# Graph-network layers on one core: VectorE adds two slots of a gathered group onto two others before TensorE sums them

## The reference

```python
msg = jnp.concatenate([h[src], h[dst]], axis=-1) @ Mw.T + Mb
deg = jax.ops.segment_sum(jnp.ones((msg.shape[0],), msg.dtype), dst, num_segments=N)
s1 = jax.ops.segment_sum(msg, dst, num_segments=N)
s2 = jax.ops.segment_sum(msg * msg, dst, num_segments=N)
mx = jax.ops.segment_max(msg, dst, num_segments=N)
mn = jax.ops.segment_min(msg, dst, num_segments=N)
mean = s1 / deg[:, None]
var = jax.nn.relu(s2 / deg[:, None] - mean * mean)
std = jnp.sqrt(var + STD_EPS)
agg = jnp.concatenate([mx, mn, std, var], axis=-1)
h_neigh = jnp.concatenate([agg, agg * (logd / DELTA), agg * (DELTA / logd)], axis=-1)
u = jnp.concatenate([h, h_neigh], axis=-1) @ Uw.T + Ub
# batch norm over nodes, mixing product, leaky ReLU, + h; then layer norm and ELU
```

## Time and profile before

| | us |
|---|---|
| median of 3 runs | 2186.88 (2179.98 to 2197.56) |
| the profiled execution, its own time | 2167.94 |
| its span, first to last instruction | 2166.1 |
| TensorE, VectorE, ScalarE, GpSimd busy | 1219.2, 710.3, 313.7, 1286.6 |

### The profile page before, as it was taken

One profiled execution on the slowest core, in us unless ns is written; L12 is line 12 of the kernel. 1 busy time (PEld: TensorE's weight loads), 2 busy tenths in 40 slices (PEclk: granted clock), 3 DMA queues, 4 the chain that ended last, 5 costly groups with the idle time before them and its releaser, 6 DMA issues.

```text
span 2166.1 us, 14665 instructions
## 1 busy us (share of the span) xinstructions
PE 1219.2 (56%) x4692; PEld 874.3 (40%) x4692; DVE 710.3 (33%) x1711; ACT 313.7 (14%) x807; POOL 1286.6 (59%) x1344
## 2 busy tenths in 40 slices
PE   6520675655546683175575637485156556646585
PEld 5310453444434452153453525353145344434452
DVE  8800423333222352042232413253033223223344
ACT  0110410110000144010100100035011000000015
POOL 2756477666766406666666666604757767667604
PEclk9995788777777796587786868697578878678798
DMA  6253233333333213323233333203323333233300
GB/s 61 70 147 92 59 97 92 89 87 94 98 84 92 61 46 115 92 85 95 88 94 94 87 95 92 86 27 116 104 73 93 94 89 96 86 92 95 92 10 30
DMA packets 88488, 183.62 MB, mean 85 GB/s; under 512 B 31790, under 2 KB 47489, under 8 KB 88409
## 3 DMA queue, kind: packets, MB, share of 16 engines
q0 software_dynamic: 61264, 164.22, 26.8%
q1 hardware_dynamic: 27150, 18.51, 3.9%
HBM read 169.06 MB, written 14.98 MB: 85 GB/s over the span
## 4 chain that ended last, share of the span: by engine, by line
another core or an unknown queue 46%; PE 28%; issue 12%; ACT 7%; DVE 5%; POOL 1%; DMA 0%; SPq 0%; DVEq 0%; ACTq 0%; POOLq 0%
PE ps L689 12%; PE ps L712 7%; PE ps L699 2%; ACT base L830 1%; PE ps L709 1%; PE ps L674 1%; PE ps L754 1%; PE ps L639 1%; PE ps L719 1%; PE ps L739 1%; ACT msq L846 1%; ACT u_sb L863 1%; ACT agg L850 0%; ACT base L828 0%
## 5 line engine op out<-in xcount | busy, mean ns | idle before, releaser
L548 POOL DMA_INDIRECT G<-p_by_rank,index x812 | 796.0, 980 | 525.6 <-issue 227.4
L689 PE MATMUL ps<-G,wide_ident 128*128 128x256 f32 x2436 | 634.6, 410 | 19.8 <-DMA G<-p_by_rank,index 12.2
L689 PEld LDWEIGHTS ps<-G,wide_ident 128*128 128x128 f32 x2436 | 499.5, 209 | 122.1 <-issue 17.5
L548 POOL DMA_INDIRECT G<-p_by_node,index x406 | 399.7, 985 | 217.5 <-issue 129.3
L712 PE MATMUL ps<-w_u_sb,aggT 128*128 128x384 f32 x600 | 266.6, 598 | 217.8 <-issue 137.0
L1261 DVE SCALAR_TENSOR_TENSOR u_sb<-ps,amp,u_sb 128x128 f32<-128x128 f32 x75 | 26.3, 351 | 824.4 <-ACT u_sb L863 599.7
L712 PEld LDWEIGHTS ps<-w_u_sb,aggT 128*128 128x128 f32 x600 | 137.9, 236 | 341.8 <-issue 200.8
L699 PE MATMUL ps<-wide_ident,agg 128*128 128x128 f32 x300 | 61.3, 339 | 339.8 <-ACT agg L850 254.2
L699 PEld LDWEIGHTS ps<-wide_ident,agg 128*128 128x128 f32 x300 | 42.2, 171 | 364.3 <-ACT agg L850 268.7
L719 PE MATMUL ps<-wide_ident,u_sb 128*128 128x128 f32 x75 | 23.8, 318 | 181.9 <-DVE u_sb L1263 101.2
L1140 DVE TENSOR_TENSOR acc<-G 128x512 f32<-128x512 f32 x150 | 96.4, 684 | 39.7 <-DMA G<-p_by_rank,index 38.5
(11 more groups left out here) (202 smaller groups left out, 1158.0 us busy)
## 6 DMA issues: line engine op xcount, KB each, us to landing
G<-p_by_rank,index POOLq DMA_INDIRECT x812
G<-p_by_node,index POOLq DMA_INDIRECT x406
p_by_rank<-base SPq DMA_DIRECT2D x12, 512.0 KB, 3.0
p_by_node<-G SPq DMA_DIRECT2D x6, 514.0 KB
w_u_sb<-in_w_u SPq DMA_DIRECT2D x3, 768.0 KB
x_r<-rows_by_rank SPq DMA_DIRECT2D x1, 1600.0 KB
windows<-src_pad SPq DMA_DIRECT2D x1, 1118.0 KB, 25.1
index<-rows_by_rank SPq DMA_DIRECT2D x1, 468.0 KB
```

Source lines behind the costliest of these rows:

```text
L548: g.indirect_dma_start(G[:, n % R, j, 0:w], None, table, bass.IndirectOffsetOnAxis(ap=index[:, t, k0 + j:k0 + j + 1], axis=0))\
L689: ins = mm(out_ps, ident[:, :], G[:, n % R, k, 0:2 * D], start=False, stop=n in END and k == nk - 1)
```

## The change

VectorE gets a new step `fold` right behind `compare`: for each group of more than two slots it adds slots 2 and 3 (or slot 2 alone of three) onto slots 0 and 1 in place, all 256 columns, once its own comparison of that group is complete. TensorE then sums at most two slots a group, and waits for the fold (`groups_folded`) before it. The first groups of a tile are folded only when the first comparison of that tile is made, which is at its second group, or at its third where the second is an odd rest (j == 1 + rest). TensorE's and ScalarE's steps at e + 4 move to e + 5, VectorE's `combine` from e + 4 to e + 5, `statistics` from e + 6 to e + 8.

```diff
--- before.py
+++ after.py
@@ -110,6 +110,7 @@
     END = {tile_groups[t][-1]: t for t in range(T)}
+    FOLD = {n: i for i, n in enumerate(n for n in range(NG) if GROUPS[n][3] > 2)}
@@ -316,6 +317,7 @@
+        folded = Signal(sem("groups_folded"), len(FOLD))
@@ -684,10 +686,13 @@
+                if n in FOLD:
+                    pe.wait_ge(folded.sem, folded.at(l, FOLD[n] + 1))
                 pe.wait_ge(gathered[n % R].sem, gathered[n % R].at(l, slot_before[n]))
-                for k in range(nk):
+                left = min(nk, 2)
+                for k in range(left):
                     ins = mm(out_ps, ident[:, :], G[:, n % R, k, 0:2 * D],
-                             start=False, stop=n in END and k == nk - 1)
+                             start=False, stop=n in END and k == left - 1)
                 ins.then_inc(pe_used.sem, 1)
@@ -720,13 +725,13 @@
-                for n in range(NG + 5):
+                for n in range(NG + 6):
                     if n < NG:
                         sums(l, n)
...
-                    if n - 4 in END:
-                        turn_update(l, END[n - 4])
+                    if n - 5 in END:
+                        turn_update(l, END[n - 5])
                     if n - 2 in END:
                         update(l, END[n - 2])
@@ -870,9 +875,9 @@
-                for n in range(NG + 5):
-                    if n - 4 in END:
-                        copy_update(l, END[n - 4])
+                for n in range(NG + 6):
+                    if n - 5 in END:
+                        copy_update(l, END[n - 5])
@@ -1161,6 +1166,20 @@
+            def fold(l, n):
+
+                t, j, _, nk = GROUPS[n]
+                own = tile_groups[t]
+                rest = GROUPS[own[1]][3] < GW
+                if j <= rest or n not in FOLD:
+                    return
+                dve.wait_ge(dve_used.sem, dve_used.at(l, n + 1))
+                for g in own[0:j + 1] if j == 1 + rest else [n]:
+                    if g in FOLD:
+                        more = GROUPS[g][3] - 2
+                        TT(G[:, g % R, 0:more, 0:2 * D], G[:, g % R, 0:more, 0:2 * D],
+                           G[:, g % R, 2:2 + more, 0:2 * D], ALU.add).then_inc(folded.sem, 1)
@@ -1274,11 +1293,11 @@
-                for n in range(NG + 7):
-                    if n - 6 in END:
-                        statistics(l, END[n - 6])
-                    if n - 4 in END:
-                        combine(l, END[n - 4])
+                for n in range(NG + 9):
+                    if n - 8 in END:
+                        statistics(l, END[n - 8])
+                    if n - 5 in END:
+                        combine(l, END[n - 5])
                     if n - 1 in END:
                         variance(l, END[n - 1])
@@ -1286,6 +1305,7 @@
                         compare(l, n)
+                        fold(l, n)
                         if n in CLOSE:
                             close(l, n)
                         if n in END:
```

## The result

The changed kernel takes 2204.97 us (median of 20 runs, 2193.05 to 2217.87) where the kernel before takes 2186.8 (20 runs beside them): ratio **1.0081, interval 1.0058 to 1.0104**. The forecast was 2147. The time went the wrong way. The change is under 1%, but with twenty runs of each kernel its interval excludes no change at all.

A forecast was written before the change was run, and what follows sets the result against it. GpSimd's gather stretches, 81% of the span, were taken as the bound, with 154 us of ring waits winnable. Terms -48 + 17 - 9 = -40 us gave 2147 us from 2186.9; range 2060 to 2240.

The forecast's parts named there:

- Fewer sums, -48: TensorE's sums: 31% fewer records make its steps less late, shrinking 154 us of GpSimd's ring waits in proportion, -48 us.
- Folds, +17: VectorE's folds beside the gathers: up to 202 us more busy time slows gathers by 0.082 us per us, +17 us.
- fourth rival: Gathers beside folds: each fold holds a gather by 0.519 us, +96 in all, 2283 us; chance 0.04.
- New waits, 0: TensorE's sums waiting for VectorE's folds at a tile's first groups: priced at 0 while GpSimd is ahead.
- third rival: A tile's first groups: folds tie TensorE to VectorE, the 154 us grow by 51, total 2246 us; chance 0.18.
- Later steps, 0: Update's turn, combination and statistics moved to later groups: 0 us of their own.
- The layer's end, -9: After a layer's last gather: 20 fewer products gain 9.9 us, ten folds partly fit idle time; -3 a layer, -9.
- second rival: Lateness of TensorE's steps: the number of products does not matter, +8 in all, 2195 us; chance 0.18.

The follow-up runs named there:

- e18: Kernel before with TensorE adding only the first slot of each group, no fold, on a chip with late TensorE steps: 2134.72 us against 2177.24, ratio 0.9815.
- e1: Kernel before with TensorE adding only the first two slots of a group, no fold, on a chip with prompt steps: 1883.78 us, ratio 0.9992.
- e13: Kernel before with TensorE adding only the first slot of each group, no fold, on a chip with prompt steps: 1886.94 us, ratio 0.9998.
- e5: The changed kernel itself, run again against the kernel before on a chip with prompt steps: 1905.23 us, ratio 1.0102.
- e3: Kernel before plus 98 fold-shaped VectorE additions a layer on data of their own, TensorE not waiting for them, prompt steps: 1899.42 us, ratio 1.0073.
- e14: Changed kernel with VectorE's running minima in PSUM, against the kernel before, prompt steps: 1884.57 us, ratio 0.9986.
- e10: Kernel before with VectorE's running maxima in PSUM for all but the last tile, prompt steps: 1886.88 us, ratio 0.9995.
- e11: Kernel before with VectorE's running minima, the second comparison of each pair, in PSUM, prompt steps: 1864.08 us, ratio 0.9873.
- e9: Changed kernel without the additions: VectorE only steps the folds' semaphore, TensorE waits for it and adds all slots; prompt steps: 1891.97 us, ratio 1.0011.
- e6: Kernel before with two slots summed a group, later steps and VectorE additions on separate data, no wait for folds, prompt steps: 1903.81 us, ratio 1.0095.
- e2: Kernel before with only the later steps, no fold, all slots summed by TensorE, prompt steps: 1885.9 us, ratio 0.9999.
- e17: Changed kernel without folds in a layer's last three tiles, ScalarE's tile 22 copy held until the layer's last gather issues, late steps: 2186.73 us, ratio 1.0009.
- e16: Changed kernel with ScalarE's copy of tile 22's turned aggregates held until the layer's last gather issues, late steps: 2202.75 us, ratio 1.0060.
- e15: Kernel before with ScalarE's copy of tile 22's turned aggregates held until the layer's last gather issues, late steps: 2192.64 us, ratio 1.0013.
- e12: Kernel before with running minima in PSUM and each tile's first minimum made by a copy to PSUM, prompt steps: 1854.65 us, ratio 0.9824.
- e8: Kernel before plus 98 VectorE additions a layer at the folds' places, of a constant to one SBUF tile, prompt steps: 1882.75 us, ratio 0.9984.

## Why the prediction was wrong

*Fewer sums, -48.* This is the step that failed: I let the lateness of TensorE's steps shrink in proportion to its records. In e18 48% fewer records left ScalarE's late steps at 986 us (939 before) and took 29 us from the stretches, where my proportion has 74. Scaled down to 31% of the records that is 29 x 31/48 = 19 us, an estimate, where steps are late; by e1 and e13 it is nothing where they are prompt. Rows 8 did order the lateness by records, weakly, as I wrote; I took the proportional value all the same. In the changed kernel even the 19 us do not show: GpSimd's waits rose by 21.

*Folds, +17.* Right in size with prompt steps: the stretches grew by 15 us (e5), the folds alone cost 13 to 21 (e3, e14). But that was luck: I priced by busy time, which e10 refutes. A fold that began ahead of a gather costs what is left of it 0.13 us after the gather's start, else nothing; over 294 folds that came to 0.05 us each, near the low end. The Trainium skill ("SBUF — State Buffer", "Who interferes with whom") has an instruction with two SBUF inputs contend with GpSimd's reads, and lets the order of issue decide which of the two blocks. The traces agree on both: a gather behind such an instruction is held to its very end, 780 times out of 780, near the boundary the instruction is lengthened instead, and 112 meetings with one input from SBUF in e11 held none. My fourth rival read that rule as a hold for every fold; in e5 87 of 294 folds held a gather, for 0.16 us in the mean. In the first pair of traces the holds did not grow (near 42 us both before and after): 9.7 us of folds came in, and other instructions of VectorE held less. That is an observation; no run shows why.

*New waits, 0.* Right with prompt steps (e9: 1.0011 with an interval from 1.0000; e6 equals e5). Where steps are late, TensorE does wait for folds (466 us, 122 of them in the second layer's gather stretch) and VectorE for the squared mean (longest wait 25.8), as the third rival has it. But GpSimd's waits rose by 21 us and not by 51. No run took the link away on a late chip, so its share there stays open.

*Later steps, 0.* Right by themselves with prompt steps (e2).

*The layer's end, -9.* Wrong in sign with prompt steps, and most likely with late ones. I counted the 20 products as gained and let the folds fit an idle place. With prompt steps the ends grow by 2 us each (e5), by additions and later steps together (e6). With late steps they grew by 10 each in the first pair of traces, and e17 against e16 puts the folds of the last three tiles at 13 us (5 to 20) of the whole time. Against that, the ends in the traces of e15 and e16 sum to 131 and 128 us. The first pair of traces overstates the growth: the span before (2166.1) lies below all timed runs of its kernel, that of after near the top of its own.

So the account of the measured +18, with late steps, is this. The folds at the layers' ends cost some 13 us (e17 against e16). All the rest comes to nothing within the noise (e17 against the kernel before: 1.0009), which must be terms that nearly cancel: fewer products, holds and waits for folds. Their sizes were not separated. With prompt steps the change costs 19 us, and the traces show it: holds +15, ends +6. The second rival (2195) came nearest to 2205 on the faster side, though it has the layer's end with the wrong sign.

Open: why TensorE's steps are late on some chips at all, whether it belongs to the chip or to something else in those runs, what the link costs there, and how e12 does there; it was run with prompt steps alone.

## What to carry over

Beside a stream of GpSimd's gathers, price a VectorE instruction by whether its two inputs lie in SBUF and whether it is already under way when a gather starts, not by its busy time. Putting one input in PSUM on the instruction that is caught won 1.3% (e11); taking nearly half the products of the sums from TensorE, which is off the path with prompt steps, won nothing (e1). An experiment that changes an instruction's inputs must keep its length and its place, or it tells nothing of the inputs (e8). A late step that no row explains should not be priced in proportion to anything: look first whether it occurs on another chip. When work is moved between engines, follow the stretch in which nothing covers the new wait.

## What the runs showed of the hardware

- The GpSimd instruction that gathers 128 rows takes 0.946 us (median of e2, e5 and after). If a VectorE instruction with two SBUF inputs began at least 0.045 us ahead of it and is under way 0.13 us after its start, it takes longer by what is left of that instruction: 780 of 780 cases in three traces, the longest gather 1.48 us (e15, L549).
- A two-input instruction that began less than 0.02 us ahead of the gather, or behind its start, held it in none of 238 cases; 27 that began between 0.02 and 0.045 us ahead and held none took 0.75 to 0.77 us themselves and not 0.69.
- With one input from PSUM (112 meetings of L1170 in e11) or a copy from SBUF to PSUM (63 in e12) the gather was never longer. For a scalar addition from SBUF to SBUF no run shows it: in e8 the 34 that met a gather with time left had begun at most 0.033 us ahead of it, and took 0.475 to 0.492 us themselves where 0.427 is usual.
- Of two equal instructions in a row, one can cost next to nothing (L1162 in e2, one gather held) and the other 0.19 us a time (L1163, 122 held), by their place against the gathers.
- The same kernel takes 1886 to 1888 us on four chips and 2177 to 2192 on two, each within 1.3% of itself. On the two, and in the first pair, ScalarE stands idle up to 38.6 us before it sees a step of TensorE, up to 34 us of that after TensorE's last product of the update had ended (874.1 to 907.9 in the trace before). In e2 no such wait exists.
- With prompt steps the mean granted clock of the whole execution was 0.722 with two products a group (e1) and 0.857 with four (e2), and both took the same time (1883.78 and 1885.9 us).
